# Attention with transposes one unit further behind the scores, and the weighted values of eight heads in one run

## The reference

```python
q, k, v = (proj(Wq, bq), proj(Wk, bk), proj(Wv, bv))      # 8 heads of 32 columns
scores = jnp.einsum('bhqd,bhkd->bhqk', q, k) * SCALE
scores = scores * (adj_matrix + bond_matrix)[:, None, :, :]
attn = jax.nn.softmax(scores, axis=-1)
ctx = jnp.einsum('bhqk,bhkd->bhqd', attn, v)
ctx = ctx.transpose(0, 2, 1, 3).reshape(b, seq_len, EMBED_DIM)
return jnp.einsum('bse,fe->bsf', ctx, Wo) + bo
```

## Time and profile before

| | |
|---|---|
| time, median of 3 runs | 2987.2 us (2986.61 to 2988.67) |
| profiled execution, span | 2986.1 us |
| TensorE busy, share of the span | 2935.2 us, 98% |
| VectorE busy | 1879.2 us, 63% |
| ScalarE busy | 1491.5 us, 50% |
| POOL busy | 720.8 us, 24% |
| masked scores (line 790) | 512 of 1219 ns |
| exponentials (line 1046) | 512 of 1147 ns |
| transposes (line 1310) | 4096 of 276 ns |

### The profile page before, as it was taken

How to read it: one execution, slowest core, us unless ns; L and a number is a source line. 1 busy time by engine, 2 the same in 40 slices (tenths; PEclk the granted TensorE clock), 3 DMA queues, 4 the chain that set the end, 5 groups by cost and what they waited for, 6 DMA issues and landing times.

```text
span 2986.1 us, 63496 instructions
## 1 busy us (share of the span) xinstructions
PE 2935.2 (98%) x23040; PEld 2371.0 (79%) x23040; DVE 1879.2 (63%) x4154; ACT 1491.5 (50%) x2761; POOL 720.8 (24%) x1305
## 2 busy tenths in 40 slices
PE   8999999999999999999999999999999999999999
PEld 7888787887878878888788886888868888688886
DVE  3797427874278742887428874388643886438863
ACT  2883317833288232873228732387323873238622
POOL 0343003420134201342013420134201341014410
PEclk9999999999999999999999999999999999999999
DMA  5202212022120231101311113111222022220200
GB/s 175 93 2 93 91 58 93 2 92 111 49 83 13 81 131 38 74 34 60 135 48 61 54 50 124 61 48 59 62 108 78 30 73 69 87 81 27 83 8 14
DMA packets 95317, 204.29 MB, mean 68 GB/s; under 512 B 10512, under 2 KB 41616, under 8 KB 94992
## 3 DMA queue, kind: packets, MB, share of 16 engines
q1 hardware_dynamic: 93456, 195.76, 17.9%
q0 software_dynamic: 1536, 4.20, 0.4%
HBM read 136.75 MB, written 8.65 MB: 49 GB/s over the span
## 4 chain that ended last, share of the span: by engine, by line
PE 68%; DVE 14%; issue 11%; POOL 4%; ACT 3%; DVEq 0%; DMA 0%; POOLq 0%; ACTq 0%; SPq 0%
PE ps L1122 39%; PE ps L1310 8%; PE ps L1403 7%; PE ps L1288 4%; PE ps L1478 4%; PE ps L1339 4%; DVE junk L832 3%; POOL H L578 3%; DVE Z L790 2%; DVE stats L629 1%; DVE h L848 1%; DVE dn L841 1%; DVE h L866 1%; POOL nm L566 1%; PE ps L1162 1%
## 5 line engine op out<-in xcount | busy, mean ns | idle before, releaser
L790 DVE CUSTOM_DVE_ANT_0 Z<-ps,adjN 128x1024 f32<-128x1024 f32 x512 | 624.0, 1219 | 69.3 <-PE ps L1288 67.1
L1046 ACT ACTIVATE Z<-Z,nm 128x1024 f32<-128x1024 f32 x512 | 587.4, 1147 | 54.2 <-POOL nm L566 54.1
L1310 PE MATMUL ps<-ident,Z 128*128 128x128 f32 x4096 | 545.9, 276 | 19.4 <-ACT Z L1046 16.9
L1310 PEld LDWEIGHTS ps<-ident,Z 128*128 128x128 f32 x4096 | 458.6, 140 | 129.4 <-issue 59.7
L1288 PE MATMUL ps<-kS,qS 128*128 128x512 f32 x1024 | 370.2, 444 | 3.3 <-issue 3.3
L578 POOL TENSOR_SCALAR H<-adjN 128x128 fp32r<-128x128 f32 (+1 forms) x456 | 316.6, 694 | 0.0
L566 POOL TENSOR_TENSOR nm<-nm,minus 128x1 f32<-128x1 f32 x512 | 97.1, 190 | 646.9 <-DVE nm L790 642.1
L1122 PE MATMUL ps<-mh,adjT 128*128 128x256 f32 x1024 | 223.6, 379 | 0.8 <-issue 0.8
L1122 PE MATMUL ps<-v,P 128*128 128x257 f32 x1024 | 223.6, 379 | 0.0
L1122 PE MATMUL ps<-hT,t3T 128*128 128x512 f32 x512 | 221.0, 592 | 0.0
L1122 PEld LDWEIGHTS ps<-v,P 128*128 128x128 f32 x1024 | 193.8, 189 | 31.9 <-issue 3.8
(11 more groups left out here) (183 smaller groups left out, 5713.5 us busy)
## 6 DMA issues: line engine op xcount, KB each, us to landing
adjT<-adjT_in SPq DMA_DIRECT2D x8, 4096.0 KB, 13.0
adjN<-adj_in SPq DMA_DIRECT2D x8, 4096.0 KB, 17.6
adjT<-adjT_in SPq DMA_DIRECT2D x8, 2048.0 KB, 7.7
qS<-qhi SPq DMA_DIRECT2D x112, 128.0 KB, 2.1
qS<-qlo SPq DMA_DIRECT2D x112, 128.0 KB, 2.1
adjT<-adjT_in SPq DMA_DIRECT2D x8, 1536.0 KB, 12.0
xn<-x_in SPq DMA_DIRECT2D x8, 1024.0 KB, 5.7
out<-x SPq DMA_DIRECT2D x8, 1024.0 KB, 4.8
```

Of the source, the lines that this page charges most:

```text
L790: dve.tensor_tensor_reduce(Z[:, u % ZS], ps[:, 2 * (u % 2):2 * (u % 2) + 2].rearrange("p a n -> p (a n)"), adjN[:, u // HEADS], SCORE_SCAL ...
L1046: act.activation(Z[:, u % ZS], Z[:, u % ZS], ACT.Exp, bias=nm[:, u:u + 1], accum_out=sm[:, u:u + 1]).then_inc(exps.sem, 1)
L1310: mm = pe.transpose(ps[:, turn_bank((u, s)), rows(a)], Z[:, u % ZS, rows(NT // 2 * s + a)], ident[:])
```

## The change

The transposes of a unit are issued one step later (BEHIND = 1), and with them both copies. Z gets a fourth buffer. The values of all eight heads of a tile are formed in one run in step 3 of the next tile, in place of four in step 7 and four in step 3; the PT slots go from eight to twelve, the signal pv_ps counts tiles in place of groups, and the last four units of a batch take other slots, so that PTa is free earlier. The four new slots (PTc) lie over qhi and qlo, so the copies of unit 8 first wait for the stacking of all queries (stacks_read). PTz moves out of adjT's region, adjT returns in two parts, and the scratch of POOL's DMAs is set to 8192 bytes. The normalisation, projection, addition and spread keep their steps; BOTH and TBANKS keep their values.

```diff
-    PTS = 8
+    PTS = 12
     PTA = 4
-    ZS = 3
+    ZS = 4
...
-                                [("PTa", [P, PTA, NT, P], F32), ("Z", [P, ZS, N], F32), ("PTz", [P, NT, P], F32)])
-        (adjT,), (PTa, Z, PTz) = adjT0, adjT1
+                                [("PTa", [P, PTA, NT, P], F32), ("Z", [P, ZS, N], F32)])
+        (adjT,), (PTa, Z) = adjT0, adjT1
+        PTz = sb("PTz", [P, NT, P])
...
-            [("stacked", [P, 4, GROUPS, N], F32), ("PTb", [P, PTS - PTA - 1, NT, P], F32), ...
+            [("keys", [P, 2 * GROUPS * N + 16], F32), ("PTc", [P, PTA, NT, P], F32), ("PTb", [P, PTS - 2 * PTA - 1, NT, P], F32), ...
...
-        BACK = (range(0, PTA), range(PTA, PTA + ZS), range(PTA + ZS, NT))
+        BACK = (range(0, PTA), range(PTA, NT))
+        BEHIND = 1
...
-            if u < UNITS:
-                turns += [(u, 0), (u, 1)]
+            if 0 <= u - BEHIND < UNITS:
+                turns += [(u - BEHIND, 0), (u - BEHIND, 1)]
...
-            slot = u % PTS
+            slot = u % PTS if u < UNITS - HPG else u % PTS + HPG
+            if slot >= 2 * PTA:
+                return PTc[:, slot - 2 * PTA]
...
-                sp.wait_ge(*pv_ps(b, NT * GROUPS - 1))
+                sp.wait_ge(*pv_ps(b, NT - 1))
...
+                    stacks_read(u)
                     dve.wait_ge(*T_ps(b, 2 * u + 2))
                     if u >= PTS:
-                        dve.wait_ge(*pv_ps(b, (u - PTS) // HPG + 1))
+                        dve.wait_ge(*pv_ps(b, (u - PTS) // HEADS + 1))
...
-                    if 2 <= u < UNITS + 2:
-                        evacuate(u - 2)
+                    if 0 <= u - 2 - BEHIND < UNITS:
+                        evacuate(u - 2 - BEHIND)
...
-                    if 1 <= u < UNITS + 1:
-                        evacuate(u - 1)
+                    if 0 <= u - 1 - BEHIND < UNITS:
+                        evacuate(u - 1 - BEHIND)
...
+                def weighted_values(t):
+                    if t == 0:
+                        pe.wait_ge(*vs(b, NT // 2))
+                    else:
+                        pe.wait_ge(*ctxs(b, t))
+                    if t < NT - 1:
+                        pe.wait_ge(*Rss(b, t + 1))
+                    for g in range(GROUPS):
+                        first = HEADS * t + HPG * g
+                        pe.wait_ge(*PT_act(b, by_act(first + HPG - 1)))
+                        for kt in range(NT):
+                            if kt == NT // 2:
+                                pe.wait_ge(*PT_dve(b, by_dve(first + HPG - 1)))
+                            for j in range(HPG):
+                                hd = ORDER[HPG * g + j]
+                                mm = pe.matmul(ps[HD * j:HD * j + HD, 7, P * g:P * (g + 1)], ...
+                    mm.then_inc(pv_ps.sem, 1)
...
-                    if u == 0:
-                        transposes(u)
                     if u + 2 < UNITS:
                         scores(u + 2)
-                    for part in range(len(PARTS)):
-                        if (g := group_due(u, WEIGH + part)) is not None:
-                            weighted_values(g, part)
+                    if (t := tile_due(u, WEIGH)) is not None:
+                        weighted_values(t)
...
-                    if 0 < u < UNITS:
-                        transposes(u)
+                    if 0 <= u - BEHIND < UNITS:
+                        transposes(u - BEHIND)
```

More of the change, by code:

```diff
@@ L157, in build_program @@
              ("W1", [P, 3, DT, D], F32)],
-            [("stacked", [P, 4, GROUPS, N], F32), ("PTb", [P, PTS - PTA - 1, NT, P], F32), ("rs", [P, HEADS, HD], F32), ("Rs", [P, GROUPS, P], F32)],
+            [("keys", [P, 2 * GROUPS * N + 16], F32), ("PTc", [P, PTA, NT, P], F32), ("PTb", [P, PTS - 2 * PTA - 1, NT, P], F32), ("rs", [P, HEADS, HD], F32), ("Rs", [P, GROUPS, P], F32)],
             [("h2", [P, NT, HID], F32), ("h2T", [P, FT, N], F32)],
@@ L166, in build_program @@
         khi, klo, qhi, qlo, hT1, W1 = p1a
-        _, PTb, rs, Rs = p1b
+        _, PTc, PTb, rs, Rs = p1b
         h2, h2T = p2
@@ L208, in build_program @@
         lasts = signal("lasts", len(LASTS))
-        adjT_back = [signal(f"adjT_back{s}", 16) for s in range(3)]
+        adjT_back = [signal(f"adjT_back{s}", 16) for s in range(2)]
         w2_in = signal("w2_in", 48)
@@ L250, in build_program @@
         PT_dve = signal("PT_dve", UNITS - NT)
-        pv_ps = signal("pv_ps", NT * GROUPS)
+        pv_ps = signal("pv_ps", NT)
         R_ps = signal("R_ps", NT)
@@ L314, in build_program @@
         INVERT, SPREAD, COPY, WEIGH, NORMALISE, PROJECT, ADD = 4, 4, 7, 7, 9, 10, 11
-        PARTS = (NT,)
         BESIDE = {1: ("v", 1), 2: ("q", KQ_FIRST + 1), 4: ("v", 2), 5: ("v", 3)}
-        BACK = (range(0, PTA), range(PTA, PTA + ZS), range(PTA + ZS, NT))
+        BACK = (range(0, PTA), range(PTA, NT))
+        BEHIND = 1
         STEPS = UNITS + HEADS + 2
@@ L495, in batch @@
                 stand(sp, waited_sp)
-                reload_adjT(2)
-                sp.wait_ge(*adjT_back[2](b, 16))
+                sp.wait_ge(*adjT_back[1](b, 16))
                 stand(sp, waited_sp)
@@ L741, in evacuate, with stacks_read @@
                     bank = turn_bank((u, 1))
+                    stacks_read(u)
                     dve.wait_ge(*T_ps(b, 2 * u + 2))
                     if u >= PTS:
-                        dve.wait_ge(*pv_ps(b, (u - PTS) // HPG + 1))
+                        dve.wait_ge(*pv_ps(b, (u - PTS) // HEADS + 1))
                     dve.tensor_copy(PT(u)[:, NT // 2:NT], heads_of(ps[:, bank])).then_inc(PT_dve.sem, 1)
+                def stacks_read(u):
+                    if u == 2 * PTA:
+                        for s in range(NH):
+                            for j in range(len(qS_in[s])):
+                                dve.wait_ge(*qS_in[s][j](b, 64))
                 def inverse_sums(t):
@@ L752, in normalise @@
                 def normalise(t):
-                    dve.wait_ge(*pv_ps(b, GROUPS * (t + 1)))
+                    dve.wait_ge(*pv_ps(b, t + 1))
                     if t == NT - 1:
@@ L1029, in evacuate @@
                 def evacuate(u):
+                    if u == 2 * PTA:
+                        for s in range(NH):
+                            for j in range(len(qS_in[s])):
+                                act.wait_ge(*qS_in[s][j](b, 64))
                     for half_of_u in range(1 + evacuates_both(u)):
@@ L1033, in evacuate @@
                         if u >= PTS:
-                            act.wait_ge(*pv_ps(b, (u - PTS) // HPG + 1))
+                            act.wait_ge(*pv_ps(b, (u - PTS) // HEADS + 1))
                         first = NT // 2 * half_of_u
@@ L1320, in spread_inverses @@
                     mm.then_inc(R_ps.sem, 1)
[L1322 to L1343, removed]
+                def weighted_values(t):
[13 more added lines that the diff above has]
+                                hd = ORDER[HPG * g + j]
+                                mm = pe.matmul(ps[HD * j:HD * j + HD, 7, P * g:P * (g + 1)],
+                                               v[:, kt, HD * hd:HD * hd + HD], PT(first + j)[:, kt],
+                                               start=(kt == 0), stop=(kt == NT - 1))
+                    mm.then_inc(pv_ps.sem, 1)
                 def project(t):
@@ L1571 @@
     arrays = {n: np.ascontiguousarray(a) for n, a in arrays.items()}
-    nc = bacc.Bacc("TRN2", target_bir_lowering=False, num_devices=1)
+    nc = bacc.Bacc("TRN2", target_bir_lowering=False, num_devices=1, dynamic_dma_scratch_size=8192)
     t = {n: nc.dram_tensor(n, a.shape, mybir.dt.from_np(a.dtype), kind="ExternalInput").ap() for n, a in arrays.items()}
```

## The result

The changed kernel takes 3030.3 us (median of 4 runs, 3028.4 to 3030.5), the kernel before 2987.9 in the same session (2986.6 to 2988.7): a ratio of 1.0142, with a 95% interval of 1.0127 to 1.0156, 42 us slower. The forecast was 3021, with 3006 to 3038 as its own range.

What follows compares the result with a forecast made beforehand. TensorE looked fullest, but a loop through VectorE, starved behind the eight-head run, was taken to bound the changed kernel: 4.2 us a batch, 33.6 in eight; 2986.1 + 33.6 + 1.1 = 3020.8, so 3021, range 3006 to 3038.

Steps and rivals of the forecast that it cites:

- Part 1: TensorE's transposes one unit further behind: gain put at 0, bounds 0.4 us a tile gained to 0.3 lost.
- the partner: Projection step: unit 5's second half needs VectorE's copy of unit 4 to free its PSUM bank; at most 0.3 us.
- The run and its edges: TensorE's eight-head values in one run: 3.65 us to the transposes behind; saved edges 0.28 us a tile.
- The saved drain: TensorE: one of two changes between 128-wide and 32-wide matmuls a tile removed, within 0.28 us of saved edges.
- The loop: Once round the tile from Z(2) over in-order queues and semaphores: period 17.24 us against 16.60, 0.64 more.
- The count: Attention of a batch: seven periods of 0.64 us plus the ends, 4.2 us a batch, 33.6 in eight.
- the ends: Start and end of a batch: -0.3 us up to the first run, +0.0 at the end.
- Covers: Stacking before unit 8's copy and adjT's two-part reload: both hidden, cost 0, at worst 2 us a batch each.
- A: TensorE stays the bound and all waits close: tile 15.9 us, 2942 us in all; chance 0.04.
- B: Only TensorE's saved change of mode counts: 18 us faster, 2969 us; chance 0.07.
- D: The later transposes gain 0.4 and the eight-head run takes it back: 2987 us; chance 0.04.
- C: Bank partner, stacking wait and reload all bite, period mid-bounds: 58 us slower, 3045 us; chance 0.07.

Runs made afterwards that it cites:

- experiment 3: Kernel before with transposes one unit further behind, values in groups of four, ScalarE copying both halves of unit 4 instead of 5: 2990.8 us, ratio 1.0007.
- experiment 4: Changed kernel with POOL's piece of the incidence moved from step 0 of a tile to step 4: 3016.2 us, ratio 1.0090.
- experiment 7: Changed kernel plus six identity transposes a tile between the halves of units 5 and 7, in seven tiles a batch: 3029.3 us, ratio 1.0141.
- experiment 2: Changed kernel with transposes and copies back at the old distance, eight heads' values still in one run: 3042.6 us, ratio 1.0181.
- the extra transposes in six tiles: Changed kernel plus six identity transposes a tile between the halves of units 5 and 7, from a batch's third tile: 3046.7 us, ratio 1.0199.

## Why the prediction was right

- **Part 1 gives nothing.** Right in its mechanism: waits for the exponential turned into waits for the copy behind it, and with the partner mended the period is 16.59 (experiment 3). I had set the partner's cost at 0, with 0.3 as a bound; alone it is 0.30 in full.
- **The run and its edges.** From its start to the transposes behind it 3.65 us were put, and 3.63 are in the trace after, where two groups were 3.78. The saved drain is real, and no time follows from it.
- **The loop.** Of its links, VectorE's copy behind the run to Z(7) measures 2.41 us (2.40 in the prediction), Z(7) to Z(0) 2.24 (2.23), Z(0) to Z(1) 1.58 (1.59), Z(1) to Z(2) 1.80 (1.86; its own terms, 1.26 and 0.58, give 1.84, so its 17.24 should read 17.22). The one that is off is Z(2) to the copy that frees the bank: 898.10 to 901.03 is 2.93 where I had 2.69, since I took POOL and ScalarE as ready for unit 2. The loop ran through unit 1, POOL's spread and its piece of the incidence instead; with the piece gone the link is 2.68 (experiment 4). That is the mis-sized term: 0.24 too little, of which the other links give back 0.06, so 17.42 for 17.24. The prediction's own sign for it, a period above 17.4, came true, though it named another copy and not POOL.
- **The count.** I took 7 periods of 0.64 less 0.3 for the ends, 4.2 us a batch. The batches are 5.1 us longer: -0.6 up to the scores of unit 8, then 0.6, four times 0.83, 0.5 (that period was 16.95 us before), 0.8 in the last units, and 0.5 behind the scores of unit 63. So the seven periods gave 5.2 for 4.5 and the ends -0.1 for -0.3. At the ends two misses nearly cancel, which is luck: the start gained 0.6 where I had 0.3, the end lost 0.5 where I had nothing. 8 x 5.1 = 41 of the 42 us.
- **Covers.** The reload was covered. The stacking did not hold the copy of unit 8: in the third batch the last transfer lands at 864.89, ScalarE copies unit 8 at 866.17 and VectorE at 866.33, neither having idled just before, and in the other seven batches the transfer is ahead of both copies as well, by 0.8 us or more. No run tried the stacking apart. The first scores to those of unit 12 take 26.5 to 28.2 us from batch to batch, 28.2 to 29.2 before. (In the kernel before, the last transfer of the third batch lands at 852.04, not near 852.7 as I had reckoned.)
- **Rivals.** A fell with experiment 7 (added work was free), B with experiment 2 (the run alone, which has the saved drain, loses 54 us), D with experiment 3. Of C, the partner was real, but with the run moving the transposes does not lose (17.42 for 17.48); that its wait is hidden there behind the loop's others is my reading, for no run moved the partner together with the run. C's price was also summed wrongly: its own terms, 0.3 x 56 = 17 for the partner and twice 16, make 33.6 + 49 = 82 us, some 3070 and not 3045.

## What to carry to other kernels

When an engine feeds another through a fixed number of PSUM banks, a longer uninterrupted piece on it starves the other for all that lies past those banks; compare the piece with what the other engine has in hand when it starts, and put work into gaps instead. Moving a consumer one step away from a producer helps only if every resource that it takes is one step further off as well: here the banks were not. And to price a change in a tightly coupled loop, go once round it over all queues, the nearly idle engine's too; the busy share of the fullest engine told nothing here.

## What was not expected of the hardware

With the extra transposes in six tiles, the time outside the attention grew from 223.1 to about 226.6 us in six of seven batches. TensorE after the jump to the next batch, in that kernel:

```profile
1155.74 0.38 PE L1175 MATMUL ps<-ident,h 128*128 128x128 f32 x2
...
1158.57 1.95 PE L1175 MATMUL ps<-ident,h 128*128 128x128 f32 x14 [2.45 <-issue]
```

and its stretches of 2 us (length, busy by engine as above, granted clock, DMA share, GB/s):

```profile
1156.00:1158.00 2.00, 0.12 (x2) 0.00 (x0) 0.93 (x4) 0.00 (x0) 0.00 (x0) 1.00 0.14 45
1158.00:1160.00 2.00, 1.43 (x13) 1.43 (x14) 0.00 (x0) 0.95 (x2) 0.00 (x0) 0.99 1.04 345
1160.00:1162.00 2.00, 2.00 (x7) 1.67 (x6) 0.00 (x0) 1.16 (x3) 0.00 (x0) 0.50 0.49 159
1162.00:1164.00 2.00, 2.00 (x7) 1.63 (x6) 0.00 (x0) 0.00 (x0) 0.00 (x0) 0.65 0.00 0
```

Two transposes of the new batch run, then TensorE stands still for 2.45 us and waits for nothing that the profile shows, and then its clock is granted at half, the 1.2 GHz level, for some 3 us. Together they cost 3.9 us in this batch. In the changed kernel the same 16 transposes run as one row (1153.00, 2.22 us). The DMA view of 1156 to 1160 us has one transfer of the queue of instructions:

```profile
q8 instruction: 1, 0.02, 1.7%
```

But the changed kernel has such a transfer too in the 5 us around its 16 transposes (1151 to 1156 us) and does not stall, so the transfer alone explains nothing. The kernel that adds 48 more of the extra transposes has neither the stall nor the slow clock (223.0 us outside the attention), and it is not slower than the changed kernel. So 17 us (3046.7 to 3029.3) went away when instructions were added, some two fifths of what the change itself cost. That TensorE waited for its instructions is one reading of a stall without a releaser beside such a transfer; no run forced it, and the cause is not shown.
